# Own instruction order for three attention iterations, double-buffered keys and values, and weight splits placed later

## The reference

```python
x = _layernorm(x + attn(x))      # 16 heads; two softmaxes per head, out = sdpa(q1,k1) - lam*sdpa(q2,k2),
                                 # rope, additive mask triu(ones), group norm over heads, then wo
x = _layernorm(x + xattn(x, ctx, ctx))   # 32 query heads, 8 key/value heads, ctx is 64 wide
x = _layernorm(x + ffn(x))       # router: top 2 of 8 experts (640 wide) + 2 shared experts
```

## Time and profile before

| | us |
|---|---|
| median of 3 runs | 905.84 |
| span of the profiled execution | 910.0 |
| first block, about | 0 to 450 |
| iteration 2, 3, 4 (from one `a_qt` copy to the next) | 26.3, 27.1, 30.8 |
| iteration 5, and most later ones | 22.9 |

### The profile page before, as it was taken

How to read it: one execution, slowest core, us unless ns; L and a number is a source line. 1 busy time by engine, 2 the same in 40 slices (tenths; PEclk the granted TensorE clock), 3 DMA queues, 4 the chain that set the end, 5 groups by cost and what they waited for, 6 DMA issues and landing times.

```text
span 910.0 us, 19793 instructions
## 1 busy us (share of the span) xinstructions
PE 778.1 (86%) x7471; PEld 502.4 (55%) x7471; DVE 585.1 (64%) x1300; ACT 512.8 (56%) x941; POOL 311.8 (34%) x481
## 2 busy tenths in 40 slices
PE   2877999999999999988689688999899999999960
PEld 1434555555555555554345345555588777877750
DVE  3455677777777777755358755868566665666533
ACT  2445577777777777774224433535355555555533
POOL 3134245555555555544200870000022222222224
PEclk9987699999999999997589899999999999999985
DMA  8118000000000000000022680515023222222325
GB/s 231 58 43 243 2 1 2 3 1 2 1 3 1 1 2 3 2 2 1 1 67 90 185 249 33 158 40 163 24 37 48 48 47 48 43 48 47 48 30 184
DMA packets 38281, 50.99 MB, mean 56 GB/s; under 512 B 9264, under 2 KB 33072, under 8 KB 38192
## 3 DMA queue, kind: packets, MB, share of 16 engines
q1 hardware_dynamic: 31040, 40.39, 15.0%
q0 software_dynamic: 7152, 9.34, 6.2%
HBM read 31.04 MB, written 18.68 MB: 55 GB/s over the span
## 4 chain that ended last, share of the span: by engine, by line
PE 33%; DVE 8%; DMA 3%; issue 2%; POOL 2%; ACT 2%; SPq 0%; ACTq 0%; POOLq 0%; DVEq 0%
PE ps L1608 29%; PE ps L1687 2%; DVE th L1495 1%; DVE wr L218 1%; DVE th L1492 1%; POOL xs L1296 1%; PE ps L1667 1%; DVE ht_lo L1500 1%; DMA acc<-y_sb,xin 1%; ACT th L1349 1%; DMA x_row<-acc 1%; DMA wst<-in_wx 1%; DVE x_row L1513 0%; PE ps L1599 0%; DMA xs<-x_row,sl 0%
## 5 line engine op out<-in xcount | busy, mean ns | idle before, releaser
L1310 POOL DMA_INDIRECT acc<-y_sb,xin x39 | 60.5, 1552 | 279.3 <-ACT y_sb L1378 279.3
L1608 PE MATMUL ps<-wr,xr_hi 128*128 x624 | 129.3, 300 | 0.0
L1608 PE MATMUL ps<-xg_hi,wsh 128*128 128x512 f16 x320 | 104.6, 389 | 5.8 <-DVE xg_lo L1485 5.8
L675 DVE TENSOR_REDUCE c_qs<-ps 128x4 f16<-128x512 f32 x128 | 83.5, 693 | 37.8 <-PE ps L933 36.2
L1349 ACT ACTIVATE th<-ps 128x384 f32<-128x384 f32 (+1 forms) x118 | 57.1, 484 | 89.4 <-PE ps L1608 77.5
L675 DVE TENSOR_REDUCE a_qs<-ps 128x4 f16<-128x512 f32 x128 | 85.3, 690 | 23.5 <-PE ps L933 22.5
L508 ACT ACTIVATE a_pt<-ps 128x512 f32<-128x512 f32 x128 | 74.7, 596 | 41.9 <-PE ps L950 39.5
L1608 PE MATMUL ps<-wr,xr_lo 128*128 x312 | 93.5, 300 | 0.0
L1492 DVE SCALAR_TENSOR_TENSOR th<-th,ps 128x384 f32<-128x384 f32 (+1 forms) x118 | 65.0, 551 | 42.3 <-ACT th L1349 34.3
L1354 ACT ACTIVATE hs<-th 128x384 f16<-128x384 f32 x78 | 36.6, 470 | 79.3 <-DVE th L1495 79.3
L508 ACT ACTIVATE c_pt<-ps 128x512 f32<-128x512 f32 x128 | 69.8, 604 | 19.4 <-PE ps L950 19.2
(11 more groups left out here) (209 smaller groups left out, 1754.0 us busy)
## 6 DMA issues: line engine op xcount, KB each, us to landing
wst<-in_wx SPq DMA_DIRECT2D x30, 640.0 KB
xs<-zero SPq DMA_DIRECT2D x1, 5031.0 KB, 23.2
xin<-xs SPq DMA_DIRECT2D x39, 129.0 KB, 2.1
acc<-x_row SPq DMA_DIRECT2D x4, 512.0 KB
x_row<-acc SPq DMA_DIRECT2D x8, 256.0 KB, 5.6
out<-x_row SPq DMA_DIRECT2D x8, 256.0 KB, 2.1
x_row<-in_x SPq DMA_DIRECT2D x1, 1536.0 KB, 10.4
wst<-in_wqkvT SPq DMA_DIRECT2D x1, 768.0 KB, 4.5
```

Of the source, the lines that this page charges most:

```text
L675: dve.tensor_reduce(t.qs[:].rearrange("p (c i) s -> p c i s", i=NI)[:, c:c + 4, f % 4, USED], score_bank(t, "m", b, f).rearrange("p (j n) ...
L1310: pool.indirect_dma_start(acc, bass.IndirectOffsetOnAxis(ap=row, axis=0), y_sb[:, n % 2, :], None, compute_op=ALU.add).then_inc(f_acc, 16)
L1608: ins = pe.matmul(o, l[x], r[y], start=(first and n == 0), stop=(last and n == m - 1), skip_group_check=not (first and last))
```

## The change

- Iterations 1, 2 and 3 get a function of their own, `first(n)`, on PE, ACT, DVE and POOL. On PE it alternates exp fill f of n-2 with max fill f of n-1. It puts `restack`, the second `back_T` and `group_mean` at the end, and in iteration 3 cross-attention's first transposes and max fills behind those. On POOL in iteration 3 `mix_sub` stands behind `cross_k_low`, `rope_sum` and the layer norm.
- Self-attention's `kt` and `v` get two buffers, so `kt_in` waits for the exp pass of two sequences before. POOL clears two more tiles at the start (`SETS` is 14 instead of 12).
- The six weight splits leave the ends of iterations 1 to 3. One stands in each of the iterations 5 to 10: the high half on ACT behind `y_high` and ahead of exp fill 4, the low half on DVE ahead of cross-attention's max fill 5.

```diff
-            t.qm, t.qt, t.kt = (sb(p + n, [P, NC, P], F16) for n in ("qm", "qt", "kt"))
-            t.v = sb(p + "v", [P, vheads, SLOTS])
+            t.qm, t.qt = (sb(p + n, [P, NC, P], F16) for n in ("qm", "qt"))
+            t.kt = [sb(p + f"kt{k}", [P, NC, P], F16) for k in range(deep)]
+            t.v = [sb(p + f"v{k}", [P, vheads, SLOTS]) for k in range(deep)]
...
@@ ACT, kt_in @@
-                if b:
-                    act.wait_ge(t.s_expfill, FILLS * b)
+                deep = len(t.kt)
+                if b >= deep:
+                    act.wait_ge(t.s_expfill, FILLS * (b - deep + 1))
...
@@ ACT, body(n), behind y_high(n - 3) @@
+                k = n - SPLIT_FROM
+                if 0 <= k < NSH * 3:
+                    split_high(act, k // 2, k % 2, wsh[:, k // 3, k % 3, 0, :])
...
@@ DVE, body(n), behind largest(C, n - 4, 4) @@
+                k = n - SPLIT_FROM
+                if 0 <= k < NSH * 3:
+                    split_low(dve, k, k % 2, wsh[:, k // 3, k % 3, 1, :], wsh[:, k // 3, k % 3, 0, :])
+                if live(n - 4):
                     largest(C, n - 4, 5)
...
@@ ACT and DVE, behind body(n) @@
-                if n <= NSH * 3 // 2:
-                    for k in range(2):
-                        e, m = divmod(2 * n - 2 + k, 3)
-                        split_high(act, n - 1, k, wsh[:, e, m, 0, :])
...
@@ POOL @@
+            def first(n):
+                q_low(n - 1)
+                k_low(n - 1)
+                if live(n - 3):
+                    group_norm(n - 3)
+                    cross_k_low(n - 3)
+                rope_sum(n)
+                if live(n - 3):
+                    power(A.mv2, A, n - 3, A.s_mv2)
+                    normalise(A.y2, A.mv2, A, n - 3, x1_ready)
+                if live(n - 2):
+                    mix_sub(n - 2)
...
@@ every engine @@
-            for n in range(ITERATIONS):
+            body(0)
+            for n in range(1, RAMP):
+                first(n)
+            for n in range(RAMP, ITERATIONS):
                 body(n)
```

More of the change, by code:

```diff
@@ L493, in kt_in @@
                 act.wait_ge(t.s_kT, b + 1)
[L494 to L496 removed]
+                deep = len(t.kt)
+                if b >= deep:
+                    act.wait_ge(t.s_expfill, FILLS * (b - deep + 1))
+                act.activation(t.kt[b % deep][:].rearrange("p c n -> p (c n)"), one.bitcast(F16), ACT.Copy
                                ).then_inc(t.s_kt_in, 1)
@@ L582, in body, with first @@
                     reqt_in(A, a_one, n - 1)
+            def first(n):
+                q_high(n - 1)
+                k_high(n - 1)
+                if live(n - 2):
+                    exp(A, n - 2, 0)
+                    exp(A, n - 2, 1)
+                kt_in(A, a_one, n - 1)
+                v_in(n - 1)
+                if live(n - 2):
+                    exp(A, n - 2, 2)
+                x_high(n)
+                if live(n - 2):
+                    exp(A, n - 2, 3)
+                if live(n - 3):
+                    y_high(n - 3)
+                if live(n - 2):
+                    exp(A, n - 2, 4)
+                    exp(A, n - 2, 5)
+                    ot_in(A, n - 2, 0)
+                    exp(A, n - 2, 6)
+                    exp(A, n - 2, 7)
+                    ot_in(A, n - 2, 1)
+                if live(n - 3):
+                    cross_k_high(n - 3)
+                reqt_in(A, a_one, n - 1)
+                if live(n - 3):
+                    cross_q_high(n - 3)
+                    kt_in(C, c_one, n - 3)
+                    qm_in(C, c_one, n - 3)
             body(0)
             setup()
-            for n in range(1, ITERATIONS):
+            for n in range(1, RAMP):
+                first(n)
+            for n in range(RAMP, ITERATIONS):
                 body(n)
-                if n <= NSH * 3 // 2:
-                    for k in range(2):
-                        e, m = divmod(2 * n - 2 + k, 3)
-                        split_high(act, n - 1, k, wsh[:, e, m, 0, :])
         @block.vector
@@ L845, in body, with first @@
                     rope_straight(n)
+            def first(n):
+                qm_in(A, a_one, n - 1)
+                largest(A, n - 1, 0)
+                largest(A, n - 1, 1)
+                largest(A, n - 1, 2)
+                x_low(n)
+                largest(A, n - 1, 3)
+                if live(n - 3):
+                    y_low(n - 3)
+                largest(A, n - 1, 4)
+                rope_free(n)
+                rope_second(n)
+                rope_first(n)
+                rope_straight(n)
+                largest(A, n - 1, 5)
+                largest(A, n - 1, 6)
+                if live(n - 3):
+                    add_self(n - 3)
+                    spread(A, A.y2, A.bn2, n - 3, A.s_add, A.s_bn2)
+                    moments(A, A.bn2, A.mv2, n - 3, A.s_bn2, A.s_mv2)
+                largest(A, n - 1, 7)
+                if live(n - 2):
+                    mix_divide(n - 2)
+                    mix_lambda(n - 2)
+                    mix_half(n - 2, 1)
+                    mix_half(n - 2, 0)
+                    spread(A, A.y, A.bn, n - 2, A.s_y, A.s_bn)
+                    moments(A, A.bn, A.mv, n - 2, A.s_bn, A.s_mv)
+                    group_in_square(n - 2)
+                    group_in_mean(n - 2)
+                    group_out(n - 2)
             body(0)
             setup()
-            for n in range(1, ITERATIONS):
+            for n in range(1, RAMP):
+                first(n)
+            for n in range(RAMP, ITERATIONS):
                 body(n)
[L851 to L854, removed]
         @block.tensor
@@ L1128, in body, with first @@
                     back_T(C, n - 4, 0)
-            for n in range(ITERATIONS):
+            def first(n):
+                if live(n - 2):
+                    exp_scores(A, n - 2, 0)
+                    exp_scores(A, n - 2, 1)
+                stack_q(A, a_one, n - 1)
+                stack_k(A, a_one, n - 1)
+                max_scores(A, n - 1, 0)
+                max_scores(A, n - 1, 1)
+                project_v(n - 1)
+                if live(n - 2):
+                    exp_scores(A, n - 2, 2)
+                max_scores(A, n - 1, 2)
+                x_T(n)
+                if live(n - 2):
+                    exp_scores(A, n - 2, 3)
+                max_scores(A, n - 1, 3)
+                if live(n - 3):
+                    y_T(n - 3)
+                if live(n - 2):
+                    exp_scores(A, n - 2, 4)
+                max_scores(A, n - 1, 4)
+                project_qk(n)
+                if live(n - 2):
+                    exp_scores(A, n - 2, 5)
+                max_scores(A, n - 1, 5)
+                if live(n - 2):
+                    values_self(n - 2, 0)
+                    exp_scores(A, n - 2, 6)
+                max_scores(A, n - 1, 6)
+                if live(n - 3):
+                    out_project(n - 3)
+                if live(n - 2):
+                    exp_scores(A, n - 2, 7)
+                max_scores(A, n - 1, 7)
+                if live(n - 2):
+                    back_T(A, n - 2, 0)
+                    values_self(n - 2, 1)
+                restack(A, a_one, n - 1)
+                if live(n - 2):
+                    back_T(A, n - 2, 1)
+                    group_mean(n - 2)
+                if live(n - 3):
+                    stack_k(C, c_one, n - 3)
+                    stack_q(C, c_one, n - 3)
+                    max_scores(C, n - 3, 0)
+                    max_scores(C, n - 3, 1)
+            body(0)
+            for n in range(1, RAMP):
+                first(n)
+            for n in range(RAMP, ITERATIONS):
                 body(n)
```

48 lines of the change are left out of this document (27 added, 21 removed).

## The result

The changed kernel takes 958.25 us (median of 4 runs, 957.56 to 960.63) against 906.15 beside it: a ratio of 1.0585 (95% interval 1.0561 to 1.0609), slower, 52 us. The profiled span is 956.1 us.

The account below looks back on a forecast made before the run. PE, issuing nearly without a gap in late iterations, was taken as the bound, at its lower clock in iterations 1 to 3. 14.4 + 20.4 - 1 + 8 = 41.8 on 905.84 gave 947 us, range 922 to 965.

Parts of the forecast that it names:

- The split's wait: Iterations 5 to 10: DVE waits for ACT's high half, delaying exp fill 5; 3.4 us a time, +20.4 us.
- The clock after the new waits: Iterations 5 to 10: lower PE clock behind four of six new waits, 2 us each; +8 us.
- the bound of 26: Upper bound of the clock term: six times the 4.3 us iteration 4 lost at half level.
- Iterations 1 to 4: The new order's cost by the end of iteration 4: +14.4 us, bounds -12 and +18.
- The handover and iteration 4: From iteration 3's restack copy to the next exp fill, +11.2 us; iteration 4's old wait goes, -3.6 us.
- The waits: PE waits for the group mean some 3 us starting iteration 3, some 5 starting iteration 4; POOL's scale chain adds 1.5.
- The sum for iteration 2: PE's work in iteration 2 added up at the lower clock: 27.9 us against 26.32, +1.6 us.
- iteration 2 no shorter than before: Sign to look for in the profile: iterations 2 and 3 are no shorter than before; under 20 us refutes.
- The double buffers: Self-attention's key copy no longer waits for exp fill 7: 0.15 us in seven iterations without a split, -1 us.
- The first: Rival: each split costs only itself, 1.0 us a time, without the wait for the high half; 925 us, chance 0.13.
- The second: Rival: lower clock in all of iterations 1 to 4 and after each new wait (+22); 965 us, chance 0.09.
- The third: Rival: pairing keeps PE at the upper clock in iterations 2 to 4, -12 us; 899 us, chance 0.05.

Follow-up runs that it names:

- experiment 1: The changed kernel with DVE's low half of each split one iteration later (6 to 11) than ACT's high half; 919.45 us.
- experiment 2: The kernel before with only the splits moved, to the changed kernel's places in iterations 5 to 10, old order and single buffers; 949.41 us.
- experiment 5: The changed kernel with 14 extra mask matmuls, results overwritten, in each of iterations 5 to 10 where PE waits for DVE; 935.31 us.
- experiment 6: The changed kernel with cross_k_high and cross stacking moved earlier in iterations 1 to 3, and split halves placed where ACT and DVE are idle; 904.85 us.
- experiment 8: experiment 6 with the new paired order in iterations 1 and 2 alone, iteration 3 in the old order; 897.18 us.
- experiment 4: The kernel before with only the double buffers of self-attention's keys and values added; 906.05 us against 904.83.
- experiment 10: experiment 6 with extra mask matmuls, results overwritten, where PE waits in iterations 1 to 3; 906.75 us against 907.36.
- experiment 7: The kernel before with only the splits moved, to iterations 5 to 10 (low halves 6 to 11) where ACT and DVE are idle; 897.83 us.
- experiment 9: experiment 7 with extra mask matmuls, results overwritten, where PE waits at the ends of iterations 1 to 3; 884.44 us.

## Why the prediction was right, and what was mis-sized

**The split's wait: right.** Forecast were 3.5 us of delay at exp fill 5, by DVE's wait for ACT; measured 3.71, six times, ended by the instructions named. 20.4 was forecast, 22.3 came; experiments 1 and 2 show the cause. PE's six stops are of 3.13 us (3.3 forecast), all ended by DVE's cross maximum.

**The clock after the new waits: the mis-sized term.** It was +8, four waits with 2 us each, by the two windows of the earlier trace rows. All six waits were followed by 1.2 GHz, at 4.1 us each: +24.7, next to the bound of 26. Experiment 5 shows it to be the clock. The forecast leaned on a wait of the second block, where matmuls of 256 columns follow; here small score tiles follow, as in iteration 4 of before, from which the bound was made. That the kind of work behind a stop makes the difference is read from these rows, and was not tested by itself.

**Iterations 1 to 4: +14.4 forecast, +5.7 measured.** The handover and iteration 4 were right: +7.6 forecast (11.2 - 3.6), +7.5 measured (38.27 instead of 30.80); the first exp fill came 12.55 us behind the restack (83.44 to 95.99), 12.9 were forecast. The waits were too: for the group mean 3.31 us in iteration 3 (some 3) and 5.71 at the handover (some 5), and 1.60 for POOL (1.5). What failed is the clock again, here in the kernel's favour. The sum for iteration 2 was made at the lower level, 27.9 us. In the profiled execution the clock rose before its end, and one of the forecast's signs, iteration 2 no shorter than before, did not come:

```profile
49.44 0.63 PE L1034 MATMUL ps<-mask,id 128*128 128x512 f16 x1
50.38 0.38 PE L1023 MATMUL ps<-a_kt,a_qm 24*128 24x128 f16 x4
50.70 1.07 PE L1054 MATMUL ps<-a_pt,a_v 128*32 128x256 f32 x16
```

and iteration 2 took 22.93 us. In experiment 6, whose PE issues the same instructions up to there, the rise did not come then:

```profile
50.45 0.63 PE L1029 MATMUL ps<-a_kt,a_qm 24*128 24x128 f16 x4
51.01 1.94 PE L1060 MATMUL ps<-a_pt,a_v 128*32 128x256 f32 x16
```

and iteration 2 took 27.06, as in experiment 5; there the sum was 0.8 too long. In experiments 1 and 8, with the same instructions, it took 22.86 and 23.16. So the moment of the rise, which differs between executions, is worth 4 us here. The Trainium skill, "TensorE: Matmul & The Clock Gate" (Part 1: The HAM clock gate), says that it differs between runs of one kernel; these rows agree. Iteration 3 took 28.99 us (+1.9 instead of +5), with the upper level from 77.5 on.

**The double buffers: -1 forecast, no gain measured,** in experiment 4; by the iterations the sign was wrong, +1.0 us over twelve of them.

**The sum.** Up to the sixteenth copy the two profiled executions differ by 53.5: 5.7 + 22.3 + 24.7 + 0.8 for the rest. The forecast of 41.8 had the clock 17 us too small and the ramp 9 too large; 958.25 lies 11 us above the 947 of the forecast and in the range. That the two errors have opposite signs is luck: with the clock's term as measured and all else as forecast the sum is 964.3, and with the split's wait (+1.9) and the rest (+1.8) as measured too it is 968, outside the range. The mechanism of the split was right; that the time fell into the range is owed in part to this.

**The rivals.** The first fell, as DVE met ACT at the same point in each of the six iterations; its kernel is experiment 1, where 1.2 us an iteration are left. The second had the lower level behind each new wait, and its price, +22, was nearer than the forecast's +8; it had the ramp wrong by 12 us. Its 965 lies 7 us from the measured time, nearer than the 947. The third, the pairing at the upper level, did not come: iteration 2 began at the lower level in every paired run (first mask 0.61 to 0.64 us). What the order would be worth at the upper level throughout no run shows. In experiment 10, the nearest to it, the ramp of 112.08 is no shorter than experiment 7's.

## What to carry to other kernels

Before moving a step into a full iteration, look where both of its halves meet: a two-engine step belongs an iteration apart, in idle stretches longer than itself (here 1.48 us of DVE's 2.11). Price a stop of TensorE at its length and at what follows it at the lower clock, taken from a stop in the same kind of work; here the second was the larger part. And where matmuls wait in a ramp, a few matmuls whose result is thrown away, in a bank that is overwritten, can be worth more than a new order (experiment 9).

## What the runs showed of the hardware that was not expected

- A stop of 3.13 us brought the clock down in each of six iterations, and one of 0.78 us in none of six; but in the ramp two stops of 1.39 and 1.12 us close together, ended at 60.06 and 61.79 in experiment 7, stood ahead of a slow stretch (granted 0.60), and so did two of 0.62 and 0.87 us, ended at 53.92 and 55.18. What tells these from the 0.78 no run shows.
- Twenty-one fillers of 512 columns in the old order's ramp were worth 13.4 us (experiment 9), though PE was already busy for 8.8 to 10 of 10 us in the slow stretches of experiment 7.
- The granted clock of a window is not always what the matmuls show. In experiment 8 it reads 0.50 from 40 to 50 us:

```profile
40.00:50.00 10.00, 10.00 (x52) 5.00 (x53) 4.25 (x8) 2.56 (x5) 0.00 (x0) 0.50 0.00 0
```

  In the changed kernel it reads 0.50 there too, but 1.00 in before and in experiment 6, while masks take 0.61 to 0.64 us in all four. In experiment 6 every window from 20 to 90 reads 1.00, with masks of 0.59 to 0.64 us up to 77.85. So the granted clock of a window is to be held against the time or the spacing of the matmuls in it.
